# A spectral convolution and group whitening on one core: second pass with the convolution expanded along the width first, and four adjacent rows of a channel on a partition

## What is computed

```
def reference(x, weight_re, weight_im, bias):        # x: 16 x 64 x 256 x 256
    x = x + spectral(gn(x), weight_re + 1j*weight_im, bias)
    return x + whiten(gn(x))

def spectral(x, w, bias):
    f = rfft2(x)                                     # only 32 x 17 low modes are kept
    f = f.reshape(B, 4, 16, fH, fW)                  # 4 heads of 16 channels
    core = einsum('bhixy,hioxy->bhoxy', f[..., :32, :17], w)
    out = zeros; out[..., :32, :17] = core
    return irfft2(out, s=(256, 256)) + bias

def whiten(x):                                       # read as rows of W = 256 features
    f = x - mean over (b, c, h)                      # one mean for each of the 256 columns
    cov = covariance of each group of 16 columns, shrunk by 1e-3, divided by (n - 1)
    return inverse(cholesky(cov)) applied to each group of 16 columns
```

## Time and profile before

| | us |
|---|---|
| median of 3 runs | 3592.57 (3587.25 to 3598.8) |
| profiled execution, its own time | 3583.13 |
| its span, first to last instruction | 3581.3 |
| mean granted TensorE clock, as a share of full speed | 0.944 |

### The profile page before, as it was taken

The page is one execution under the profiler, slowest core; times in us unless marked ns, Lnnn a source line. Parts: engine busy times, 40 slices in busy tenths (PEclk is TensorE's granted clock), DMA queues, the critical chain, the costliest instruction groups (busy, mean ns, idle before and its releaser), DMA issues.

```text
span 3581.3 us, 219711 instructions
## 1 busy us (share of the span) xinstructions
PE 3040.3 (85%) x92677; PEld 1916.8 (54%) x92677; DVE 2540.9 (71%) x4358; ACT 1230.0 (34%) x2860; POOL 1167.6 (33%) x1690
## 2 busy tenths in 40 slices
PE   5888888888886432566699999999999999999999
PEld 3555555555554431222466666666666666666665
DVE  3777777777777327555577777777777777777777
ACT  1222222222221321000355555555555555555554
POOL 3666666666665114454011111111111111111111
PEclk7999999999998555899799999999999999999999
DMA  9999999999998660998488888888888888888888
GB/s 227 324 327 331 329 328 329 329 328 329 329 325 238 87 91 2 299 355 284 166 293 293 293 292 293 293 293 292 293 293 293 292 293 293 293 292 293 293 293 275
DMA packets 761328, 1001.86 MB, mean 280 GB/s; under 512 B 103712, under 2 KB 464176, under 8 KB 761264
## 3 DMA queue, kind: packets, MB, share of 16 engines
q1 hardware_dynamic: 659888, 912.51, 79.9%
q10 hardware_dynamic: 101376, 88.39, 8.5%
HBM read 639.46 MB, written 361.28 MB: 279 GB/s over the span
## 4 chain that ended last, share of the span: by engine, by line
PE 71%; ACTq 8%; issue 7%; DMA 6%; DVE 5%; SPq 2%; ACT 1%; DVEq 0%; POOL 0%; POOLq 0%
PE bank L583 15%; PE bank L576 15%; PE bank L598 14%; PE bank L566 6%; ACTq L642 6%; PE bank L421 5%; DMA reg<-xh_d 5%; PE bank L432 4%; PE bank L440 3%; PE bank L454 2%; PE bank L501 2%; PE bank L525 1%; SPq L293 1%; ACT xh L634 1%; PE bank L463 1%
## 5 line engine op out<-in xcount | busy, mean ns | idle before, releaser
L634 ACT ACTIVATE reg<-bank 128x512 f32<-128x512 f32 (+3 forms) x1696 | 927.7, 578 | 1061.5 <-PE bank L583 910.9
L1046 DVE STREAM_TRANSPOSE reg<-bank 128x256 f32<-128x256 f32 x2048 | 739.0, 419 | 388.7 <-PE bank L598 388.7
L750 POOL TENSOR_TENSOR reg<-reg 128x512 f32<-128x512 f32 x512 | 689.1, 1346 | 443.2 <-PE bank L432 390.8
L1050 DVE SCALAR_TENSOR_TENSOR reg<-reg,m,mwhit 128x1024 f32<-128x1024 f32 x512 | 657.7, 1284 | 72.2 <-DVE reg L1046 38.2
L803 POOL TENSOR_TENSOR reg<-reg,tab 128x64 f32<-128x64 f32 x512 | 164.4, 321 | 1556.9 <-PE bank L598 1546.0
L576 PE MATMUL bank<-tab,reg 128*128 128x128 f32 x4096 | 561.7, 279 | 20.5 <-issue 20.5
L583 PE MATMUL bank<-reg,tab 34*128 34x512 f32 x2048 | 579.1, 642 | 0.0
L836 DVE TENSOR_TENSOR reg<-reg 128x512 f32<-128x512 f32 x512 | 530.6, 1036 | 53.0 <-DMA reg<-in_x_dram 27.6
L598 PE MATMUL bank<-reg 32*32 32x128 f32 x32768 | 546.6, 279 | 1.7 <-DVE reg L1046 1.7
L576 PEld LDWEIGHTS bank<-tab,reg 128*128 128x128 f32 x4096 | 441.7, 140 | 131.1 <-ACT reg L634 103.6
L598 PEld LDWEIGHTS bank<-reg 32*32 32x32 f32 x32768 | 362.8, 103 | 218.7 <-issue 172.4
(11 more groups left out here) (119 smaller groups left out, 1700.4 us busy)
## 6 DMA issues: line engine op xcount, KB each, us to landing
reg<-in_x_dram SPq DMA_DIRECT2D x256, 1024.0 KB, 8.3
reg<-in_x_dram SPq DMA_DIRECT2D x512, 512.0 KB, 3.9
out_dram<-reg SPq DMA_DIRECT2D x512, 512.0 KB, 3.0
xh_d<-xh ACTq DMA_DIRECT2D x128, 512.0 KB
reg<-xh_d SPq DMA_DIRECT2D x128, 512.0 KB, 5.8
gram_d<-gram ACTq DMA_DIRECT2D x64, 256.0 KB
reg<-gram_d SPq DMA_DIRECT2D x64, 256.0 KB, 4.8
spec_d<-psu ACTq DMA_DIRECT2D x512, 8.5 KB
```

Source lines behind the costliest of these rows:

```text
L634: copy = lambda o, i, **k: nc.scalar.activation(o, i, ACT.Copy, **k)
L750: nc.gpsimd.tensor_tensor(out=halves[:, q % 2, 1], in0=x_in[:, 2 * q:2 * q + 2, 0], in1=x_in[:, 2 * q:2 * q + 2, 1], op=ALU.subtract).then ...
L1046: ins = v.transpose(o_sb[:, q].rearrange("p n (f w) -> p f n w", f=2)[:, :, :, BL * j:BL * j + BL], bank[4 + j][:, 0:W].rearrange("p (f n ...
L1050: v.scalar_tensor_tensor(out=o_sb[:, q], in0=o_sb[:, q], scalar=m1[:, ds(t * 4 + q, 1)], in1=mwhit[:, :].unsqueeze(1).to_broadcast([P, 4, W]),
```

## The change

The convolution is now expanded along the width first and along the height last, and the layout of a pair changes: partition = channel (2) x 64, each with four adjacent rows of the image, 4 KB long in DRAM. So in the second pass:

- the load and the store move pieces of 4 KB, as many bytes as before;
- the eight transposes of 128x128 become sixteen of 64 rows by 128 columns, taken in turn from the lower and the upper 64 partitions (channel 0 and channel 1), each giving 64 columns; bank 2 now holds channel 0 and bank 3 channel 1. The first of the sixteen is an ordinary product with the unit matrix, the rest are transposes;
- all sixteen wait for both copies of the pair before;
- the products that add the convolution have 64 rows and 256 columns, four of them in place of two of 512 columns, and the wait for whitening stands between the third and the fourth;
- the spectra of two pairs are laid side by side, transposed by one 128x128 transpose (`spectrum_turned`) and expanded along the width by two products (`widened`), once for two pairs in place of two products for each pair; ScalarE keeps the transposed spectrum (128x128) on even q and the expanded one (128x512) on odd q.

```diff
-        v_sb, a = cut(big, a, 2, 2, W)
-        xt_sb, a = cut(big, a, 2, 2, 512)
+        ct_sb, a = cut(big, a, 2, P)
+        z_sb, a = cut(big, a, 2, 2, W)
+        xt_sb, a = cut(big, a, 2, 2, 2, H)
...
-            def expand(t, q):
-                pe.wait_ge(*nth("cs_ready", t * 4 + q + 1))
-                pe.wait_ge(*nth("v_ready", t * 4 + q))
-                for c in range(2):
-                    r = slice(KH * c, KH * c + KH)
-                    ins = mm(bank[c][:, 0:H], cs[r, q].rearrange("p a b -> p (a b)"), T("hb")[r], **one)
-                ins.then_inc(S["v_mm"], 1)
+            def spectrum_turned(t, m):
+                pe.wait_ge(*nth("cs_ready", t * 2 + m + 1))
+                pe.wait_ge(*nth("z_ready", t * 2 + m))
+                mm(bank[0][:, W:W + P], cs[:, m].rearrange("p a b -> p (a b)"), T("eye"), start=True, stop=True,
+                   is_transpose=True).then_inc(S["ct_mm"], 1)
+            def widened(t, m):
+                pe.wait_ge(*nth("ct_ready", t * 2 + m + 1))
+                for e in range(2):
+                    r = slice(KH * e, KH * e + KW)
+                    ins = mm(bank[e][:, 0:W], ct_sb[r, m], T("e0")[r], **one)
+                ins.then_inc(S["z_mm"], 1)
...
-                for half in range(2):
-                    pe.wait_ge(*nth("xt2_copied", t * 8 + 2 * q + half - 1))
-                    for c in range(2):
-                        for r in range(2):
-                            ins = mm(bank[2 + half][:, H * c + P * r:H * c + P * r + P],
-                                     x_re[:, 2 * q + c, r, P * half:P * half + P], T("eye"), start=c == 0 and r == 0,
-                                     stop=False, is_transpose=True, skip_group_check=True)
+                pe.wait_ge(*nth("xt2_copied", t * 8 + 2 * q))
+                for half in range(2):
+                    for r in range(4):
+                        for c in range(2):
+                            at = H * half + KH * r
+                            k = slice(KH * c, KH * c + KH)
+                            ins = mm(bank[2 + c][:, at:at + KH], x_re[k, q, r, P * half:P * half + P], T("eye")[k, k],
+                                     start=half == 0 and r == 0, stop=False, is_transpose=half + r + c > 0, skip_group_check=True)
...
-                    r = slice(KH * half, KH * half + KW)
-                    mm(bank[2 + half][:, :], T("ey")[r], v_sb[r, q % 2].rearrange("p c h -> p (c h)"),
-                       start=False, stop=True, skip_group_check=True).then_inc(S["xt2_mm"], 1)
+                    for c in range(2):
+                        k = slice(KH * c, KH * c + KH)
+                        if half == 1 and c == 1 and before is not None:
+                            may_whiten(*before)
+                        ins = mm(bank[2 + c][:, H * half:H * half + H], z_sb[k, q // 2, q % 2, P * half:P * half + P],
+                                 T("hb")[k], start=False, stop=True, skip_group_check=True)
+                        if half == 1:
+                            ins.then_inc(S["xt2_mm"], 1)
...
+                    if q % 2 == 0 and ahead:
+                        spectrum_turned(*ahead)
+                    turn(t, q, before)
+                    if q % 2 == 1 and ahead:
+                        widened(*ahead)
+                    if before:
+                        whitened(*before)
...
-            def kept(t, q):
-                act.wait_ge(*nth("v_mm", t * 4 + q + 1))
-                act.wait_ge(*nth("xt2_mm", t * 8 + 2 * q - 2))
-                copy(v_sb[:, q % 2], low[:, :, 0:H]).then_inc(S["v_ready"], 1)
+            def turned_kept(t, m):
+                act.wait_ge(*nth("ct_mm", t * 2 + m + 1))
+                act.wait_ge(*nth("z_mm", t * 2 + m - 1))
+                copy(ct_sb[:, m], bank[0][:, W:W + P]).then_inc(S["ct_ready"], 1)
+            def widened_kept(t, m):
+                act.wait_ge(*nth("z_mm", t * 2 + m + 1))
+                act.wait_ge(*nth("xt2_mm", t * 8 + 4 * m - 4))
+                copy(z_sb[:, m], low[:, :, 0:W]).then_inc(S["z_ready"], 1)
...
-                        kept(*((t, q + 2) if q < 2 else (t + 1, q - 2)))
+                        (turned_kept, widened_kept)[q % 2](*((t, 1) if q < 2 else (t + 1, 0)))
```

More of the change, by code:

```diff
@@ L70, in tables @@
     put("wj", wj.reshape(2 * KY, 2, P).transpose(2, 1, 0))
-    put("hb", hk_row.reshape(P, P, 2).transpose(0, 2, 1))
-    for half in range(2):
-        put("ey", (cj[:, None] * wj)[:, P * half:P * half + P], slice(KH * half, KH * half + KW))
-    put("e0", cj[:, None] * wj, slice(0, KW))
+    put("hb", hk_row.reshape(P, H // 4, 4).transpose(0, 2, 1))
+    for e in range(2):
+        put("e0", cj[:, None] * wj, slice(KH * e, KH * e + KW))
     put("e1", cj[:, None] * wj, slice(1, KW + 1))
@@ L135, in whiten_kernel @@
     x_v = x.rearrange("b c (t p) w -> p (b c) t w", p=P)
-    x2_v = x.rearrange("b c (p t) w -> p (b c) t w", p=P)
-    out_v = out.rearrange("b c (p t) w -> p (b c) t w", p=P)
+    x2_v = x.rearrange("b (n c) (p t) w -> (c p) (b n) (t w)", c=2, t=4)
+    out_v = out.rearrange("b (n c) (p t) w -> (c p) (b n) (t w)", c=2, t=4)
     xh_d = nc.dram_tensor("xh_d", (NU, P, PAIRS, W), f32, kind="Internal").ap()
@@ L248, in whiten_kernel @@
             ms_mm ms_ready mw_mm mw_ready
[L249 removed]
+            cs_zero cs_ready w_scaled w_ready x_re_in0 x_re_in1 x_re_in2 x_re_in3 ct_mm ct_ready z_mm z_ready xt2_mm xt2_copied o_mm wd_ready o_turned o_ready x_re_used0 x_re_used1 x_re_used2 x_re_used3
             out_stored0 out_stored1 out_stored2 out_stored3""".split()
         HEAD = dict(sync={},
[L254 removed]
+                    tensor=dict(x_used0=1, x_used1=1, x_used2=1, x_used3=1, q_half=2, q_mm=2, ct_mm=2, z_mm=2, z_ready=1, xt2_mm=4, o_mm=2, o_turned=1,
                                 x_re_used0=1, x_re_used1=1, x_re_used2=1, x_re_used3=1, xh_mm=2),
@@ L571, in turn @@
+            def widened(t, m):
+                pe.wait_ge(*nth("ct_ready", t * 2 + m + 1))
+                for e in range(2):
+                    r = slice(KH * e, KH * e + KW)
+                    ins = mm(bank[e][:, 0:W], ct_sb[r, m], T("e0")[r], **one)
+                ins.then_inc(S["z_mm"], 1)
+            def turn(t, q, before=None):
                 pe.wait_ge(*nth(f"x_re_in{q}", t * 16 + 16))
+                pe.wait_ge(*nth("xt2_copied", t * 8 + 2 * q))
                 for half in range(2):
-                    pe.wait_ge(*nth("xt2_copied", t * 8 + 2 * q + half - 1))
@@ new lines, in turn @@
+                ins.then_inc(S[f"x_re_used{q}"], 1)
+                pe.wait_ge(*nth("z_ready", t * 2 + q // 2 + 1))
+                for half in range(2):
+                    for c in range(2):
+                        k = slice(KH * c, KH * c + KH)
[5 more added lines that the diff above has]
+                            ins.then_inc(S["xt2_mm"], 1)
@@ L606, in four @@
                 for q in range(4):
[L607 to L615, removed]
+                    before = (t, q - 1) if q >= 1 else (t - 1, 3) if not first else None
+                    ahead = (t, 1) if q < 2 else (t + 1, 0) if not last else None
+                    if q % 2 == 0 and ahead:
[4 more added lines that the diff above has]
+                    if before:
                         whitened(*before)
-            expand(0, 0)
-            expand(0, 1)
+            spectrum_turned(0, 0)
+            widened(0, 0)
             four(0, first=True)
@@ L720, in four @@
                     act.wait_ge(*nth("o_mm", t * 4 + q - 1))
-                    for half in range(2):
-                        act.wait_ge(*nth("xt2_mm", t * 8 + 2 * q + half + 1))
-                        copy(xt_sb[:, q % 2, half], bank[2 + half][:, :]).then_inc(S["xt2_copied"], 1)
+                    for c in range(2):
+                        act.wait_ge(*nth("xt2_mm", t * 8 + 2 * q + c + 1))
+                        copy(xt_sb[:, q % 2, :, c], bank[2 + c][:, :].rearrange("p (f h) -> p f h", f=2)
+                             ).then_inc(S["xt2_copied"], 1)
                     if not (last and q == 3):
@@ L726, in four @@
                     if not (last and q >= 2):
-                        kept(*((t, q + 2) if q < 2 else (t + 1, q - 2)))
+                        (turned_kept, widened_kept)[q % 2](*((t, 1) if q < 2 else (t + 1, 0)))
             scaled(0, 0)
-            for q in range(2):
-                kept(0, q)
+            turned_kept(0, 0)
+            widened_kept(0, 0)
             with act.Fori(0, NP // 4 - 1) as t:
@@ L789, in _, with spectrum_of @@
             pool.wait_ge(*nth("cs_zero", 1))
[L790 to L793, removed]
+            def spectrum_of(t, m):
+                pool.wait_ge(*nth("ct_mm", t * 2 + m - 1))
+                nc.gpsimd.tensor_copy(cs[:, m, :, 0:KW], C[:, ds(t * 4 + 2 * m, 2)]).then_inc(S["cs_ready"], 1)
             def four(t, last=False):
                 for q in range(4):
-                    if not (last and q >= 2):
```

(5 more changed lines are left out.)

21 lines of the change are left out of this document (8 added, 13 removed).

## The result

The changed kernel takes **3546.98 us** in the median (3543.96 to 3551.07, 4 runs) against 3592.93 of the kernel before; the ratio is 0.9866, 95% interval 0.9847 to 0.9885. It is 46 us faster. The forecast was 3695, slower; the time lies in the range only because rival 3 was let into it.

The account below looks back on a forecast made before the run. TensorE was taken to bound the second pass; 3.29 + 3.52 for two pairs plus waits of 0.23 and 0.52 gave 7.56, or 3.78 us a pair against 3.58, +102 us over 512 pairs: 3695, range 3515 to 3815.

Parts of the forecast that it names:

- rival 3: Second pass: half-price transposes, stage 0.54 us, VectorE the bound at 6.87 for two pairs, 3520; chance 0.18, shared with covered waits.
- What bounds the kernel: Second pass before the change: TensorE decides, waiting for nobody, 3.58 us for a pair.
- The transposes: Second pass: sixteen 64-row transposes take nine load slots of 0.103 us; the stage stays 1.03 us.
- The bound "about 0.54": Transpose stage: its length in us if the 64 streamed columns decided instead of the 128 of the load.
- The prediction's last line: Signs of being wrong: TensorE waits for nobody in the second pass, or its transposes take 0.6 or 1.8 us.
- The two halves of the array work side by side: TensorE's transposes: two loads in different halves run together, so sixteen need eight double slots and a ninth.
- Convolution, expansion: Second pass: convolution stays 0.96 us a pair; expansion products, 0.43 us, made once for two pairs.
- The waits: TensorE waits for ScalarE's copies: 0.23 us from even to odd pair, 0.52 from odd to even.
- The wait for VectorE: Ahead of the convolution's last product: met 2.55 us after whitening starts, load due at 2.80, so no cost.
- Rivals 1 and 2: Transpose stage: more drains, +0.2 us a pair, about 3800, chance 0.13; halves not overlapping, +0.82, 4115, chance 0.08.
- Rival 4: About nothing: waits half as long as worked out, 3.59 us a pair, within 11 us of before; chance 0.06.
- Pieces of 4 KB cost and give nothing: Second pass loads and stores: 4 KB pieces cost nothing, as no engine waits for a transfer.

Follow-up runs that it names:

- e1: Kernel before, its eight transposes made as ordinary products with only 64 columns of the unit matrix (half of each transpose left out): 4054.61 us.
- e2: Kernel before, its eight transposes made as ordinary products with all 128 columns of the unit matrix: 4072.85 us.
- e10: Changed kernel with all sixteen transposes of a pair made as ordinary products with the unit matrix: 4123.5 us.
- e12: Changed kernel with three of VectorE's four block transposes of a pair (a quarter of the output left out): 3550.4 us.
- e9: Changed kernel with each load of a pair split in two, pieces of 2 KB, stores unchanged: 3549.3 us.
- e5: Changed kernel with the odd pair's expansion along the width between its transposes and convolution, and ScalarE copying that result first: 3448.07 us.
- e6: Changed kernel with the odd pair's expansion along the width between its transposes and convolution, ScalarE's copy order unchanged: 3658.2 us.

## Why the prediction was wrong

- **What bounds the kernel** (TensorE, waiting for nobody): right for the kernel before.
- **The transposes, "The stage is then 1.03 us, as before": this is the step that failed.** It measured 0.59. With 0.59 for 1.03 twice, the prediction's own sum for two pairs falls from 7.56 to 6.68, of 6.96 measured; the 3.78 us a pair, and with it the sign, rested on this term. "The transposes follow the loads" took a pace of 0.103 us for the load's, but at 128 streamed columns the two candidates cannot be told apart. e1, e2 and e10 show that 0.11 is indeed the pace of an *ordinary* load whatever its rows, and the change's own trace and the second load of the kernel before show 0.06 for a transpose's. The bound "about 0.54" was close. The prediction's last line had named a stage of 0.6 as a sign that it is wrong. The section "LDWEIGHTS (loading the stationary operand)" of TensorE: Matmul & The Clock Gate in the Trainium skill, P / 1.2, holds for the ordinary loads here (0.11 against its 0.107) and for 64 rows too, but not for transposes (0.06). The prediction's "the trace's 103 agrees" compared it with a pace that wasn't a load's.
- **The two halves of the array work side by side**, taken from the 64-row products: right for transposes as well.
- **Convolution, expansion**: the convolution's products stream as before. From its first product to whitening an even pair takes 1.13 (2406.81 to 2407.94) and not 0.96 + 0.10, which the wait behind it hides. The expansion is made once for two pairs, as worked out.
- **The waits**: right in place and in cause. 0.23 and 0.52 were predicted, 0.24 (whitening 2407.94 to transposes 2409.18, less 1.00) and 0.30 (2411.66 to 2412.96) came. The second is smaller because VectorE holds TensorE back in the odd pair just before, which shortens that wait without shortening the pair, as e12 showed from the other side.
- **The wait for VectorE, "met with 0.2 to spare, and costs nothing while TensorE is as slow as I expect"**: with transposes at 0.59 it isn't met in the odd pair, as the condition said. The 0.4 us that it holds up there cost nothing even so, as ScalarE's loop hides them (e12).
- **Rival 3** has the right mechanism, half-price transposes: 6.87 us for two pairs, 72 us gained, 3520. It named VectorE as the bound, at 6.87. That loop is indeed about 6.9, but the one that sets the measured 6.96 is ScalarE's, which I had at 6.58; that the two came out so close, and the rival's time with them, is partly luck. Of the 0.38 by which ScalarE's loop is longer than I had it, 0.05 lies in each of the two transpose stages (0.59 for 0.54) and 0.08 in each of the two first copies, which start 1.24 us behind the convolution's first product and not 1.16 (2408.05 against 2406.81); the rest, about 0.12, is for the most part the start behind a wait (0.14 from the copy's end at 2412.82 to 2412.96, where I had 0.04). The rival's chance of 0.18 was too low: the text gave it "nothing" for evidence, and the evidence stood in the same trace.
- **Rivals 1 and 2** both needed a stage longer than 1.03 and fall with the 0.59. Rival 4 kept the stage at 1.03 as well.
- **Pieces of 4 KB cost and give nothing**: right for the loads, within e9's interval. The stores weren't tested.

Of the second pass's 54 us the profiled execution kept 32, as the middle took 21 more, and the medians differ by 46.

## What to carry to other kernels

When two limits would give the same pace (here 128 columns loaded and 128 streamed), a row that shows the pace says nothing on which it is; look at the first instructions of the group, which have nothing ahead of them to wait for: there the two separate. When an edit removes a visible wait and nothing gets faster, look for a second loop of nearly the same length before giving up on it: here two edits worth +53 and +3 us alone were worth -110 together. And order the short copies of an engine by who waits for them: e5 and e6 differ in nothing else, and by 210 us.

## What the runs showed of the hardware

- A float32 transpose on TensorE takes a slot of 0.11 us with 128 rows and 128 streamed columns and of 0.06 with 64 and 64, with the clock granted at 1.00; that the columns set it, and not the rows, is argued above. Its load of 128 columns takes no more than 0.06, where the load of an ordinary float32 product takes 0.11 (e1, e2, e10), for 128 rows as for 64.
- Sixteen transposes of 64 rows, taken in turn from the two halves of the array, take 0.59 us where eight of 128 rows took 1.03, for the same numbers transposed.
- With loads of 2 KB for 4 KB pieces, in twice as many transfers, the DMA share rises from 0.85 to 0.90 at the same 301 GB/s (e9).
